# Saving the scan's carried state on GpSimd instead of VectorE in a fused scan and feed-forward kernel

## The reference, cut to what matters

```
xn    = layernorm(x)                                   # x: 16 x 2048 x 2048
xz    = xn @ W_xproj.T                                 # delta_r (128) | B (16) | C (16)
delta = softplus(delta_r @ W_dt.T + b_dt)
dA    = exp(delta[..., None] * A);  Bu = delta[..., None] * B * xn[..., None]
h[t]  = dA[t] * h[t-1] + Bu[t]                         # 16 states for each of 2048 channels
y[t]  = sum_n h[t, n] * C[t, n];  attn = y + xn * D_param
ffn   = relu(xn @ sign(up_w).T) @ sign(down_w).T * down_scale * output_scale
out   = x + attn + ffn
```

## Time and profile before

| what | us |
|---|---|
| median of three runs | 10095.83 (10085.98 to 10099.13) |
| the profiled execution | 10092.04, span of its slowest core 10091.0 |
| spans of the eight cores | 10043.6 to 10091.0 |
| DVE busy | 7670.9 (76%) |
| POOL busy | 5502.0 (55%) |
| PE busy | 4957.4 (49%) |
| ACT busy | 2878.9 (29%) |

### The profile page before, as it was taken

The page is one execution under the profiler, slowest core; times in us unless marked ns, Lnnn a source line. Parts: engine busy times, 40 slices in busy tenths (PEclk is TensorE's granted clock), DMA queues, the critical chain, the costliest instruction groups (busy, mean ns, idle before and its releaser), DMA issues.

```text
span 10091.0 us, 71302 instructions; the slowest of 8 cores (10043.6 to 10091.0 us)
## 1 busy us (share of the span) xinstructions
PE 4957.4 (49%) x17832; PEld 1997.3 (20%) x18176; DVE 7670.9 (76%) x7267; ACT 2878.9 (29%) x4151; POOL 5502.0 (55%) x2948
## 2 busy tenths in 40 slices
PE   2152243256624565256743666246752577336662
PEld 1021111122211222112211222112221222112221
DVE  3364356598885988679885989869885888859887
ACT  4333332223222232232322232132322323222221
POOL 2242244366663666466663666646663666636665
PEclk7576676578866887578765676667775677657776
DMA  4656554122202221112211222122211122122221
GB/s 130 168 162 191 159 182 142 61 67 94 82 32 79 77 96 67 65 52 86 100 46 67 71 96 73 35 76 80 98 65 59 59 90 98 38 71 80 73 73 50
DMA packets 255815, 880.03 MB, mean 87 GB/s; under 512 B 29296, under 2 KB 29552, under 8 KB 242992
## 3 DMA queue, kind: packets, MB, share of 16 engines
q1 hardware_dynamic: 181680, 674.08, 20.1%
q10 hardware_dynamic: 73728, 201.36, 6.7%
HBM read 774.66 MB, written 100.66 MB: 87 GB/s over the span
## 4 chain that ended last, share of the span: by engine, by line
DVE 49%; issue 18%; POOL 13%; DMA 10%; ACT 5%; PE 4%; DVEq 1%; ACTq 1%; SPq 0%; POOLq 0%
DVE h L679 26%; POOL Bu L647 12%; DVE w L403 7%; DVE w L413 5%; DMA stg<-dnw 4%; DVE y L415 3%; DMA stg<-upw 3%; DMA x_t<-x 3%; DVE y L354 2%; DVE u L616 2%; ACT sgn L221 2%; DVE w L375 1%; POOL w L375 1%; DVEq L138 1%; DMA out<-out_t 1%
## 5 line engine op out<-in xcount | busy, mean ns | idle before, releaser
L647 POOL TENSOR_TENSOR Bu<-u,bct 128x512 f32<-128x512 f32 x2048 | 2944.1, 1450 | 4540.3 <-DVE u L616 3220.6
L679 DVE TENSOR_TENSOR_SCAN h<-dA,h,Bu 128x512 f32<-128x512 f32 x2048 | 3794.8, 1868 | 564.5 <-POOL Bu L647 561.4
L303 PE MATMUL ps_hid<-xn_d,wup 128*128 128x512 bf16 x8032 | 2383.2, 462 | 2501.6 <-ACT hid L319 1685.1
L636 ACT ACTIVATE dA<-delta,negA 128x512 f32<-128x512 f32 x2048 | 1465.4, 720 | 5483.1 <-DVE h L679 5450.3
L338 PE MATMUL ps_dn<-hid,wdn 128*128 128x512 bf16 x8024 | 2154.8, 430 | 1282.0 <-DVE y L354 1056.0
L375 POOL TENSOR_TENSOR w<-h,bct 128x1024 f32<-128x1024 f32 x896 | 2609.6, 2913 | 0.0
L303 PEld LDWEIGHTS ps_hid<-xn_d,wup 128*128 128x128 bf16 x8192 | 911.8, 114 | 3952.5 <-issue 3646.2
L338 PEld LDWEIGHTS ps_dn<-hid,wdn 128*128 128x128 bf16 x8192 | 867.5, 108 | 2548.5 <-issue 2145.6
L616 DVE TENSOR_TENSOR u<-delta,xn_d 128x512 f32<-128x512 f32 x256 | 174.8, 683 | 1250.3 <-ACT delta L597 1250.2
L403 DVE TENSOR_TENSOR w<-w 128x512 f32<-128x512 f32 x512 | 915.9, 1789 | 2.2 <-issue 1.4
L405 DVE TENSOR_TENSOR y<-y,w 128x512 f32<-128x512 f32 x512 | 597.2, 1166 | 54.3 <-DVE w L403 1.4
(11 more groups left out here) (46 smaller groups left out, 1732.0 us busy)
## 6 DMA issues: line engine op xcount, KB each, us to landing
wup<-scr_up SPq DMA_DIRECT2D x512, 512.0 KB, 4.2
wdn<-scr_dn SPq DMA_DIRECT2D x512, 512.0 KB, 4.6
x_t<-x SPq DMA_DIRECT2D x96, 1024.0 KB, 6.3
stg<-upw ACTq DMA_DIRECT2D x128, 512.0 KB, 5.4
stg<-dnw ACTq DMA_DIRECT2D x128, 512.0 KB, 5.7
scr_up<-sgn ACTq DMA_DIRECT2D x128, 256.0 KB, 4.2
scr_dn<-sgn ACTq DMA_DIRECT2D x128, 256.0 KB, 4.1
out<-out_t SPq DMA_DIRECT2D x128, 256.0 KB, 2.1
```

Of the source, the lines that this page charges most:

```text
L303: instr = TE.matmul(ps_hid[:, (gidx % 2) * 512:(gidx % 2 + 1) * 512], wup[:, (gidx % 2) * 2048 + dk * 128:(gidx % 2) * 2048 + (dk + 1) * 128],
L636: inc(SC.activation(dA_t[:, aslot * TT:(aslot + 1) * TT], dslot, AF.Exp, scale=negA[:, ncol:ncol + 1]), s_s)
L647: inc(PO.tensor_tensor(Bu_t[:, aslot * TT:(aslot + 1) * TT], u_t[:, pslot * TT:(pslot + 1) * TT], bct[:, nl * TT:(nl + 1) * TT], ALU.mult) ...
L679: inc(VE.tensor_tensor_scan(h_t[:, hslot * TT:(hslot + 1) * TT], dA_t[:, aslot * TT:(aslot + 1) * TT], Bu_t[:, aslot * TT:(aslot + 1) * TT ...
```

## The change

The two 128x1 copies after every second scan are issued on POOL instead of DVE. They raise s_p instead of s_v, and POOL waits for the scan ahead of them. The waits that referred to the copies follow: the memset of h0 and the scans wait on s_p, and a scan that overwrites an h slot waits until the copy has read it.

```
-                wait(VE, "v", s_v, m.get(("h0done", k - 1), 0))
+                wait(VE, "v", s_p, m.get(("h0done", k - 1), 0))
...
                     if nl < 4:
-                        if s >= 1:
-                            en, val = m[("wm", k, s - 1, (nl + 4) // 2)]
+                        pk, ps2 = (k, s - 1) if s >= 1 else (k - 1, 31)
+                        if pk >= 0:
+                            en, val = m[("wm", pk, ps2, (nl + 4) // 2)]
                             if en == "p":
                                 wait(VE, "v", s_p, val)
...
+                            wait(VE, "v", s_p,
+                                 m.get(("h0cp", pk, ps2, (nl + 4) // 2), 0))
                     else:
...
+                        wait(VE, "v", s_p,
+                             m.get(("h0cp", k, s, (nl - 4) // 2), 0))
-                    wait(VE, "v", s_v, m.get(("h0c", ncol), 0))
+                    wait(VE, "v", s_p, m.get(("h0c", ncol), 0))
...
                     if nl % 2 == 1:
-                        wait(VE, "v", s_v, m[("scan", k, s, nl)])
-                        inc(VE.tensor_copy(h0[:, ncol - 1:ncol],
+                        wait(PO, "p", s_v, m[("scan", k, s, nl)])
+                        inc(PO.tensor_copy(h0[:, ncol - 1:ncol],
                                            h_t[:, (hslot - 1) * TT + TT - 1:
-                                               (hslot - 1) * TT + TT]), s_v)
-                        inc(VE.tensor_copy(h0[:, ncol:ncol + 1],
+                                               (hslot - 1) * TT + TT]), s_p)
+                        inc(PO.tensor_copy(h0[:, ncol:ncol + 1],
                                            h_t[:, hslot * TT + TT - 1:
-                                               hslot * TT + TT]), s_v)
-                        m[("h0c", ncol - 1)] = s_v.n - 1
-                        m[("h0c", ncol)] = s_v.n
+                                               hslot * TT + TT]), s_p)
+                        m[("h0c", ncol - 1)] = s_p.n - 1
+                        m[("h0c", ncol)] = s_p.n
+                        m[("h0cp", k, s, (nl - 1) // 2)] = s_p.n
...
-                m[("h0done", k)] = s_v.n
+                m[("h0done", k)] = s_p.n
```

## The result

The changed kernel takes 10603.55 us (median of 8 runs, 10591.08 to 10613.68) against 10097.61 us for the kernel before on the same chip (8 runs, 10085.98 to 10108.05). The ratio is 1.0501, 95% interval 1.0489 to 1.0512: slower by 506 us. The forecast was 10650, slower, with a range of 10330 to 10950. Two more executions of the changed kernel, 10597.64 and 10661.10 us, are not among the eight and would not move the median.

What follows compares the result with a forecast made beforehand. The prediction took a lock shared by DVE and POOL, almost never free, as the bound. 228 steps x 2.6 = +593 us, less 39 in tile 0, gave +554 on 10092.04, stated as 10650 us; range 10330 to 10950.

Steps and rivals of the forecast that it cites:

- tile 0: Steps with weight preparation, where ACT sets the pace: u to scan 5 shortens by 1.4 us in 28 steps, -39 us.
- The lock: Resource shared by DVE and POOL: their operations run one after the other, and it is free for next to no time.
- waits: latency and lost overlap: POOL starts 0.14 us after each of three scans; five POOL operations lose 0.20 each, four DVE additions 0.14 each.
- eight copies on POOL: The moved copies in POOL's row, taken at 0.15 us each, with 0.10 and 0.40 as ends.
- copies gone from DVE: Only the pair after scan 7 is on the path, saving 0.23 us a step; the other pairs are covered by products.
- laid down 2.8: New order of the step listed instruction by instruction with durations: next u at 34.1 against 31.31 us, +2.8.
- The mean of +2.6 us a step: Mean of +2.8 and +2.4 for the two kinds of step; over 228 remaining steps +593 us.
- The lower bounds: Copies at 0.10 and no loss on DVE: 1.9 a step, about 10490; without any loss of overlap: 1.3, 10350.
- The upper bound: Copies on POOL at 0.40 us each: eight add 2.0 more, 4.6 us a step, 11100 us.
- Dear copies: Rival: a copy on POOL costs 0.5 us or more, 5.4 us a step, 11290 us; 7%.
- The cheap case: Rival: copies don't take the lock, no loss of overlap; +0.8 to +1.3 a step, 10230 to 10350 us; 17%.
- Faster: Rival: POOL's reordering finds room, copies vanish at no cost, the pair after scan 7 is saved; 10000 us; 5%.

Runs made afterwards that it cites:

- the last kernels: Kernel before with all products and w on DVE: copies on DVE 9125.55 us, on ACT 8889.19 us, on POOL 8883.18 us.
- waits only: Kernel before, copies still on DVE, with POOL made to wait for the second scan of each pair before its next w or product: 10411.00 us, ratio 1.0321.
- deferred copies: Kernel before with the copies moved to POOL, each pair two products later in POOL's row than in the change: 10087.32 us, ratio 0.9995.
- ACT kernel: Kernel before with the copies moved to ACT, each pair behind the dA that has waited for the same scan: 9895.29 us, ratio 0.9802.

## Why the prediction was right, point by point

**A slip of names first.** The prediction calls the step from 3239.78 "even" and the next one "odd", and so do the headings of the earlier trace rows. The indices are the other way round: it is s = 3. POOL's row that is shown above for "an even step" is that of an odd one too. The fourth w of an odd step is run at the start of the next, even one, which is why the even step has the w on DVE. The durations belong to the rows shown, and each kind is half of the steps, so the sum is untouched.

**What was right.** The mechanism held: the change costs by waits in POOL's row that hold back w and the products, and the sum's terms for them were near what was measured. The total came out closer than its parts, by luck: the steps were forecast about 100 us too dear, and 34 of the 39 us in tile 0 didn't come.

**The lock is never free.** The experiments bear it out: in the last kernels fewer operations meet, and they are faster although DVE gets more work (all products and w on DVE, 9125.55 us).

**The ledger of a step**, for s = 3, in us:

| term | forecast | measured | from |
|---|---|---|---|
| waits: latency and lost overlap | 0.42 + 1.56 | 1.70 | waits only, 33.01 - 31.31 |
| eight copies on POOL | 1.20 | 0.72 | changed, 33.73 - 33.01 |
| copies gone from DVE | -0.23 | 0, within the above | below |
| sum | 2.95, laid down 2.8 | 2.42 | 33.73 - 31.31 |

The latency of 0.14 us held (0.13 from scan to copy), and the cold durations came out as laid down: w 2.13 and two products 2.27 us, against 2.12 and 2.26. Of the 0.53 us between 2.95 and 2.42, about half (0.28) lies in the waits; which of the nine amounts of lost overlap was too much was not worked out, but of the four additions counted one, L405 at 3267.56, ran alone at 0.69 us already before. The other half (0.25) lies in the copies with DVE's saving. One copy shows 0.18 us as busy time, more than my 0.15, but the next operation starts 0.12 to 0.14 us after it (3342.06, 3342.18, 3342.32), and the first pair costs nothing, since it falls between the two additions (L403 ends 3336.75, L405 starts 3336.86 and takes its lone 0.69). That leaves three pairs of 0.26 us ahead of w, 0.78.

The saving of 0.23 us was a wrong step in two ways. In the kernel before, the copies cost 0.79 us in this step, not 0.23. The prediction took the pair after scan 5 for covered, since "the next scan needs that product". It doesn't: the product that starts at 3262.75 is number 7, and scan 6 needs number 6, which began at 3259.27 and ended at 3260.87. Scan 6 was ready and stood behind product 7 at the lock. And in the changed kernel nothing of it is collected at the place I named, since w2 now stands behind scan 7 and the addition waits for w2 in any case. With the waits alone, copies still on DVE, the addition after scan 7 waits 2.05 us for w.

**The mean of +2.6 us a step** was measured as 2.11: 2.31 for the kind shown first and 1.92 for the other, forecast 2.8 and 2.4.

**The lower bounds** mix two bases. "A step loses 1.9" follows from the ledger's 2.95 (less 0.56 and 0.40); from the mean of 2.6, which the sum uses, it is 1.6, and about 10430 us. Without any loss of overlap it is 1.0 and not 1.3, about 10290. The upper bound, 4.6, does start from 2.6. The result lies far from both.

**Tile 0** failed. The mechanism was there: in its 28 steps with weight preparation, the time from u to the last dA fell by 47 us (core 0: 632.6 to 585.4), more than the forecast 39. But from that dA to the next u, which is the preparation with its DMAs, it grew by 52, 41 and 29 us on cores 0, 3 and 6. Over all cores, 5 us are left of the 39. The waits-only kernel has the same 50 us up to the last dA and gave back only 11 to 17. Most of the growth, 42, 30 and 18 us on these cores, is longer idle time ahead of ACT's sign operations (L221), which wait for the weights' DMAs. Why those came later isn't known, and no experiment was made on it.

**Between the tiles** I had forecast the ordinary loss of a step. It was 5.5 us each, 39 in all: 2.2 in the last step, about as forecast, 2.8 in writing the tile out (first to last L446, mean of eight cores: 39.3 to 42.1 us; on core 6 40.4 to 43.8) and 0.6 before the next u, where nothing was moved. This stretch and tile 0 vary between kernels: with deferred copies they are about 22 and 40 us longer than before (mean of eight cores), though that kernel's steps are shorter. That is why its steps gain 0.35 us each and its total nothing. It stays open.

**The sum**, from the starts of u, mean over eight cores: 203 steps x 2.11 = +428, the first and sixteenth steps +28, between the tiles +39, the end of tile 0 +4, its preparation -5, together +494. Of the remaining 12 of the 506 us, 5 lie behind the last u; the rest is the difference between the mean over the cores of one execution and the median of the slowest cores. Forecast: +593 - 39 = +554. The steps with their share between the tiles were forecast 20% too dear (593 against 495), and most of the 39 us of tile 0 didn't come.

**The rivals.** Dear copies fell with the deferred copies, which cost nothing on balance. The cheap case, in which copies don't hold the lock, is half true: a copy on POOL is held up by DVE (1.03 us in place of 0.18), but the rows read here show no case in which it held up DVE; still the waits decide. "Faster" asked for the next product to keep its place under a DVE operation; the deferred and the ACT kernel leave POOL's products there, and their steps are 0.35 and 0.96 us shorter.

**Offloading between the two engines.** That it might not help (the Trainium skill, Perfetto Trace Analysis, section "Optimizing Scalar/DVE Operations") fits this change, +506 us, but not as a rule on copies: with w and products off POOL the same offload gained 242 us. For a POOL instruction the Trainium skill (GPSIMD Engine Reference, section "Instruction dispatch") names one indirect call of tens of cycles, from which my estimate was under 0.1 us. The runs show a spacing of 0.12 to 0.14 us: a little over that estimate, and a little under my 0.15.

## What to carry to other kernels

Where two engines take turns as here, count time under the lock, not busy time. In these kernels an operation was better placed on the engine that holds the lock for the shorter time, even though that engine was already the busiest, and falling busy shares went with a longer run. A tiny instruction put into an in-order queue costs what its wait does to everything behind it; put it behind the operations that are ready already, or on an engine whose queue has waited for the same event. A copy that looks hidden in a timeline may still decide who gets the lock next, so take it out once before you price it.

## What the runs showed of the hardware that I had not expected

Copies of 128x1 on POOL didn't measurably slow DVE's two-input operations in the kernel that has nothing else on POOL: DVE's busy time is 6910.9 us with the copies on POOL and 6910.0 with them on ACT. POOL's copies are held up meanwhile to a mean of 752 ns, against 0.18 us where nothing holds them:

```profile
L410 POOL COPY h<-h 128x1 f32<-128x1 f32 x2048 | 1477.2, 752 | 7353.8 <-DVE h L701 7353.8
```

On ACT the same copy takes 181 ns. Two dependent copies on DVE between a scan and the next operation cost 0.30 us, though each shows 0.15 us and they overlap by half.
